# Storing a tile one step ahead of its neighbour's loads, and reordering maxima, rounding and latents at the start of an int8 stage

## The reference

```python
x = x + L0_ffn(L0_cond(x))                       # x1
y = conv(x, weight, groups=4, pad=4) + ctx + bias
outlier = any(abs(y) > 6, axis=rows)              # per column
row_absmax = max(abs(where(outlier, 0, y)), axis=1)
Cx = round(where(outlier, 0, y) * 127 / row_absmax)
out = Cx @ CB.T * (row_absmax / 127) * (SCB / 127) + outlier part + bias
x = x + out                                       # x2
```

## Time and profile before

| | us |
|---|---|
| median of three runs | 1683.25 |
| the runs | 1673.1, 1683.25, 1688.26 |
| the profiled execution | 1679.22 |
| its span, first to last instruction | 1677.5 |

### The profile page before, as it was taken

The page is one execution under the profiler, slowest core; times in us unless marked ns, Lnnn a source line. Parts: engine busy times, 40 slices in busy tenths (PEclk is TensorE's granted clock), DMA queues, the critical chain, the costliest instruction groups (busy, mean ns, idle before and its releaser), DMA issues.

```text
span 1677.5 us, 20601 instructions
## 1 busy us (share of the span) xinstructions
PE 1583.9 (94%) x7752; PEld 1289.1 (77%) x7752; DVE 833.7 (50%) x1318; ACT 506.1 (30%) x761; POOL 312.6 (19%) x262
## 2 busy tenths in 40 slices
PE   7898777999999879998999999999999999999996
PEld 5787546988987558886888888887878888888875
DVE  4666368986475545773333333333733333333336
ACT  4443223343336541223222222212242222222112
POOL 1000011134326550021311101112012111111110
PEclk9999898999999999999999999999999999999998
DMA  8765423556675667795271111112924411111115
GB/s 303 215 191 165 131 75 114 179 177 222 201 246 163 248 216 262 274 377 172 84 141 41 48 50 50 50 51 75 360 93 103 98 50 50 50 50 50 51 38 175
DMA packets 117240, 238.56 MB, mean 142 GB/s; under 512 B 22503, under 2 KB 61551, under 8 KB 115778
## 3 DMA queue, kind: packets, MB, share of 16 engines
q1 hardware_dynamic: 82042, 155.27, 27.8%
q0 software_dynamic: 23008, 68.24, 13.7%
q10 hardware_dynamic: 12112, 14.00, 2.8%
HBM read 164.51 MB, written 89.19 MB: 151 GB/s over the span
## 4 chain that ended last, share of the span: by engine, by line
PE 76%; DVE 5%; POOL 2%; issue 2%; DMA 2%; ACT 1%; SPq 0%; ACTq 0%; DVEq 0%; POOLq 0%
PE pu L1924 26%; PE pd L1924 25%; PE l_po L1924 6%; PE pf L1924 6%; POOL scratch_pairs L1433 2%; PE pw L640 2%; PE pw L639 2%; PE l_ea L1286 2%; PE l_ea L1857 1%; PE l_po L1857 1%; PE pg L1066 1%; PE l_tr L1872 1%; DMA delta<-scratch_expert_out 1%; PE l_ea L1872 1%; DVE y1T L942 1%
## 5 line engine op out<-in xcount | busy, mean ns | idle before, releaser
L1924 PE MATMUL pd<-down_hi,hid_hi 128*128 128x512 f32 x640 | 249.2, 389 | 2.9 <-issue 2.9
L1924 PE MATMUL pu<-y_hi,up_hi 128*128 128x512 f32 x640 | 249.3, 389 | 0.0
L1924 PE MATMUL pu<-y_lo,up_hi 128*128 128x512 f32 x640 | 249.1, 389 | 0.0
L1924 PE MATMUL pd<-down_hi,hid_lo 128*128 128x512 f32 x640 | 249.0, 389 | 0.0
L1924 PE MATMUL pd<-down_lo,hid_hi 128*128 128x512 f32 x640 | 249.0, 389 | 0.0
L1924 PE MATMUL pu<-y_hi,up_lo 128*128 128x512 f32 x640 | 249.0, 389 | 0.0
L2225 DVE TENSOR_TENSOR hid_lo<-hidden,hid_hi 128x512 fp32r<-128x512 f32 x64 | 44.3, 692 | 388.2 <-ACT hid_hi L2133 388.2
L2055 POOL TENSOR_TENSOR down_lo<-raw,down_hi 128x1024 fp32r<-128x1024 f32 x40 | 100.3, 2508 | 678.4 <-ACT down_hi L2070 678.4
L2127 ACT ACTIVATE hidden<-pu 128x512 f32<-128x512 f32 x64 | 38.3, 598 | 467.6 <-PE pu L1924 467.6
L2164 DVE TENSOR_TENSOR acc<-pd,acc 128x512 f32<-128x512 f32 x224 | 143.6, 685 | 54.8 <-PE pd L1924 51.5
L1924 PEld LDWEIGHTS pd<-down_hi,hid_hi 128*128 128x128 f32 x640 | 120.2, 188 | 28.6 <-issue 3.7
(11 more groups left out here) (317 smaller groups left out, 2508.7 us busy)
## 6 DMA issues: line engine op xcount, KB each, us to landing
X<-scratch_x SPq DMA_DIRECT2D x256, 64.0 KB, 2.5
l_x<-scratch_x SPq DMA_DIRECT2D x32, 512.0 KB, 6.3
delta<-scratch_expert_out SPq DMA_DIRECT2D x32, 512.0 KB, 6.9
raw<-in_up SPq DMA_DIRECT2D x32, 512.0 KB, 3.7
raw<-in_down SPq DMA_DIRECT2D x32, 512.0 KB, 4.5
y1T<-in_x SPq DMA_DIRECT2D x16, 512.0 KB, 9.6
scratch_x<-y1T SPq DMA_DIRECT2D x16, 512.0 KB, 3.2
scratch_x<-l_x SPq DMA_DIRECT2D x16, 512.0 KB, 5.6
```

The source lines that it names most:

```text
L1924: mm = pe.matmul(out, lhs[a], rhs[b], start=first and n == 0, stop=last and n == len(pairs) - 1)
```

## The change

On SP, the loop of the first stage stores tile s and only then loads the windows of tile s - 1. For tiles 14 and 15 SP loads the even pieces, ScalarE the odd ones. At the int8 stage, `row_peaks` has two `tensor_tensor` maxima in place of one `tensor_reduce`; group 0's magnitudes have room for both halves; tile 0 is scaled, rounded and split before tile 1 is rounded, into buffers of its own for tile 1 (`z_one`); group 1's magnitudes and first maxima stand earlier; 16 of the 32 latent units stand behind tile 0's, 1's and 2's products. The slots of `x2` are swapped, and GpSimd waits for the first `z_lo`.

```diff
@@ phase_first, sync @@
-            for t in range(NT):
-                sp.wait_ge(x1_made, 2 * (t + 1))
-                sp.dma_start(SC["x1"][t], x[:, t, :]).then_inc(x1_stored[t % 4], 16)
-                for c in SPLIT_AT.get(t, ()):
-                    sp.wait_ge(turned, 2 * (c + 1))
-                    x_in(LEAD + c)
-                sp.wait_ge(x1_stored[t % 4], 16 * (t // 4 + 1))
...
-                load_windows(sp, SC["x1"], t, X[t % XS], X_loaded[t % XS])
+            for s in range(NT + 1):
+                if s < NT:
+                    sp.wait_ge(x1_made, 2 * (s + 1))
+                    sp.dma_start(SC["x1"][s], x[:, s, :]).then_inc(x1_stored[s % 4], 16)
+                    for c in SPLIT_AT.get(s, ()):
+                        sp.wait_ge(turned, 2 * (c + 1))
+                        x_in(LEAD + c)
+                t = s - 1
+                if t >= 0:
+                    sp.wait_ge(x1_stored[t % 4], 16 * (t // 4 + 1))
...
+                    load_windows(sp, SC["x1"], t, X[t % XS], X_loaded[t % XS], range(0, KC, 1 if t < NT - 2 else 2))
@@ phase_first, scalar @@
                     act.copy(whT[:], pm[:, 2 * P:3 * P]).then_inc(whT_made, 1)
+                t = {NT - 1: NT - 2, NT + 1: NT - 1}.get(s)
+                if t:
+                    act.wait_ge(x1_stored[t % 4], 16 * (t // 4 + 1))
+                    act.wait_ge(conv_done, 2 * (t - XS + 1))
+                    load_windows(act, SC["x1"], t, X[t % XS], X_loaded[t % XS], range(1, KC, 2))
@@ phase_l1 @@
+    z = [buf["z_one"] if t == 1 else buf["z"][t % 2] for t in range(NT)]
...
+    PEAKS = 5
+    whole = [KC * t + KC if t < GROUPED[0][1] else KC * (GROUPED[0][1] + group_of[t]) for t in range(NT)]
@@ gpsimd @@
+        pool.wait_ge(z_lo, 1)
@@ scalar: magnitudes @@
-            if i:
-                act.wait_ge(peaked, 3 * g + 1)
-            elif g:
-                act.wait_ge(peaked, 3 * g - 1)
+            if g:
+                act.wait_ge(peaked, PEAKS * g + 2 if i else PEAKS * g - 1)
+            m0 = n * i if g == 0 else 0
@@ scalar, in program order @@
-        ahead["war"](act)
         act.wait_ge(kept, 2)
         magnitudes(0, 0)
+        magnitudes(0, 1)
+        ahead["war"](act)
         latent_out(0)
+        magnitudes(1, 0)
         latent_out(1)
-        magnitudes(0, 1)
         latent_out(2)
+        high(0)
+        high(1)
         latent_out(3)
-        latent_out(4)
-        high(0)
-        latent_out(5)
         for s in range(NT):
-            if s == 0:
+            if s == 1:
+                latent_out(4)
+                latent_out(5)
+            if s == 2:
                 latent_out(6)
-                latent_out(7)
...
+            if s == 2:
+                latent_out(7)
-            if s + 1 < NT:
+            if 1 <= s < NT - 1:
                 high(s + 1)
@@ vector: row_peaks @@
-            dve.tensor_reduce(peak[:, i, 0:n, :].unsqueeze(3), mag[:, 0:n, :, :].rearrange("k t p j -> k t j p"), AX.X,
-                              ALU.max).then_inc(peaked, 1)
+            half = mag[:, n * i:n * i + n, :, :] if g == 0 else mag[:, 0:n, :, :]
+            at = PEAKS * g + 2 * i
+            dve.tensor_tensor(half[:, :, 0:2, :], half[:, :, 0:2, :], half[:, :, 2:4, :], ALU.max).then_inc(peaked, 1)
+            dve.wait_ge(peaked, at + 1)
+            dve.tensor_tensor(peak[:, i, 0:n, :], half[:, :, 0, :], half[:, :, 1, :], ALU.max).then_inc(peaked, 1)
@@ vector, in program order @@
-        scale(0, 0, 4)
-        round_(0, 0, KC)
+        scale(0, 0, 1)
+        round_(0, 1)
+        scale(0, 1, 2)
         low(0)
+        round_(1, 1)
+        row_peaks(1, 0)
+        low(1)
@@ tensor @@
-        latent(0, 13)
+        latent(0, 6)
         turn(0)
-        latent(13, 18)
+        latent(6, 10)
         broadcast(0)
-        latent(18, 32)
+        latent(10, 16)
...
+            if s == 2:
+                latent(28, 32)
...
+            if s == 0:
+                latent(16, 19)
+                broadcast(1)
+                latent(19, 24)
+            if s == 1:
+                latent(24, 28)
```

More of the change, by code:

```diff
@@ L641, in conv_windows, with load_windows @@
     return last
-def load_windows(sp, dram, t, dst, sem):
+def load_windows(sp, dram, t, dst, sem, parts=range(KC)):
     view = dram.rearrange("t (n c) (p k) -> t p c n k", n=2 * GROUPS, p=KC)
-    for p in range(KC):
+    for p in parts:
         sp.dma_start(dst[p * GI:(p + 1) * GI, :, :], view[t, p]).then_inc(sem, 16)
@@ L729, in phase_l1 @@
     base_hi, base_lo = K["l2_base"]
-    x1, x2, bias, z, y2, stage, mag, peak, row, tmp, pf, pv, pt, pb, pg = [buf[n] for n in (
-        "x1 x2 bias z y2 stage mag peak row tmp pf pv pt pb pg").split()]
+    x1, x2, bias, y2, stage, mag, peak, row, tmp, pf, pv, pt, pb, pg = [buf[n] for n in (
+        "x1 x2 bias y2 stage mag peak row tmp pf pv pt pb pg").split()]
+    z = [buf["z_one"] if t == 1 else buf["z"][t % 2] for t in range(NT)]
     gout, g_stored = K["g_out"], K["g_stored"]
@@ L743, in phase_l1 @@
     LATE = 8
+    PEAKS = 5
     group_of = [g for g, (t0, n) in enumerate(GROUPED) for _ in range(n)]
-    first = {t0: g for g, (t0, n) in enumerate(GROUPED)}
+    whole = [KC * t + KC if t < GROUPED[0][1] else KC * (GROUPED[0][1] + group_of[t]) for t in range(NT)]
     def store_y2(sp, t):
@@ L876, in scalar @@
                     g = group_of[s] + 1
-            if g and j == 0:
+            if g and j == 0 and s:
                 magnitudes(g, 0)
@@ L935, in scale, with round_ @@
                                   pb[:, j * P:(j + 1) * P].unsqueeze(1).to_broadcast([P, KC, P]), ALU.mult).then_inc(scaled, 1)
-        def round_(g, p0, p1):
-            t0, n = GROUPED[g]
+        def round_(t0, n):
             dve.wait_ge(scaled, t0 + n)
-            for p in range(p0, p1):
+            for p in range(KC):
                 part = y[:, t0:t0 + n, p, :]
@@ L947, in low @@
                 dve.wait_ge(f_mm, 2 * (t - 1))
-            dve.wait_ge(rounded, KC * (group_of[t] + 1))
-            dve.tensor_tensor(z[t % 2][1][:], y[:, t, :, :], z[t % 2][0][:].bitcast(F32), ALU.subtract).then_inc(z_lo, 1)
+            dve.wait_ge(rounded, whole[t])
+            dve.tensor_tensor(z[t][1][:], y[:, t, :, :], z[t][0][:].bitcast(F32), ALU.subtract).then_inc(z_lo, 1)
         def add(t, h):
@@ L954, in add @@
                 dve.wait_ge(xb, t + 1)
-                if t == 0:
-                    dve.wait_ge(g_mm, KC)
+                if t == 1:
+                    dve.wait_ge(g_mm, 6)
                 if t >= 2:
@@ L959, in add @@
             dve.wait_ge(f_mm, 2 * t + h + 1)
-            dve.scalar_tensor_tensor(out=x2[:, t % 2, half], in0=pf[h][:], scalar=row[:, t:t + 1], in1=K["scb_row"][:, half],
+            dve.scalar_tensor_tensor(out=x2[:, (t + 1) % 2, half], in0=pf[h][:], scalar=row[:, t:t + 1], in1=K["scb_row"][:, half],
                                      op0=ALU.mult, op1=ALU.mult).then_inc(x2_part, 1)
             dve.wait_ge(x2_part, 2 * t + h + 1)
-            dve.tensor_tensor(x2[:, t % 2, half], x2[:, t % 2, half], x1[:, t % 2, half], ALU.add).then_inc(x2_made, 1)
+            dve.tensor_tensor(x2[:, (t + 1) % 2, half], x2[:, (t + 1) % 2, half], x1[:, t % 2, half], ALU.add).then_inc(x2_made, 1)
         dve.tensor_reduce(cmax[:].unsqueeze(2), K["top"][:].rearrange("p t k -> p k t"), AX.X, ALU.max).then_inc(kept, 1)
@@ L1031, in turn @@
             t0, n = GROUPED[g]
[L1032 removed]
+            pe.wait_ge(peaked, PEAKS * (g + 1))
             if g:
@@ L1051, in product @@
             for k in range(KC):
-                last = split_product(pe, pf[h][:], [v[:, k, :] for v in z[t % 2]],
+                last = split_product(pe, pf[h][:], [v[:, k, :] for v in z[t]],
                                      [K["cbT"][:, k, h * HALF:(h + 1) * HALF]], k == 0, k == KC - 1)
@@ L1101, in tensor @@
                 turn(g)
-            if g and ((n == 2 and j == 0) or (n == 4 and j == 1)):
+            if g and n == 4 and j == 1:
                 broadcast(g)
@@ L2382, in build @@
         phase_first(nc, K, A, SC)
+        z_one = [place(nc, UPPER, f"z_one_{part}", 194496 + 4 * D * i, [P, KC, P], F32R) for i, part in enumerate(("hi", "lo"))]
         with ExitStack() as both:
```

32 lines of the change are left out of this document (15 added, 17 removed).

## The result

The changed kernel takes 1659.7 us (median of 4 runs, 1654.3 to 1664.4) beside 1681.1 for the kernel before (4 runs, 1673.1 to 1688.3). The ratio is 0.9873, 95% interval 0.9844 to 0.9903: a gain of 21.4 us, from 16.3 to 26.2. The forecast was 1653, or 28 less, within 1640 to 1668. The sign and the places were right, the size nearly 7 us too large.

A forecast was written before the change was run, and what follows sets the result against it. TensorE, busy 94%, bounds the kernel; gains come from its waits and low clock at two seams. First seam 10.8, second 16.2, later maxima 1 sum to 28.0 off 1679.2: 1651.2, or 1655.3 by the median; forecast 1653, range 1640 to 1668.

The forecast's parts named there:

- First seam, the tail (12.3): End of the first stage: SP's tile period stops being the limit, convolution 15 moves from 191.3 to 179.0, 12.3 us gained.
- the new wait: Before convolution 12: its copy stands behind ScalarE's four loads of tile 14, a wait of some 3 us.
- nothing or 2.2: First seam: possible loss in us to the lower clock if the wait before convolution 12 brings a slow start.
- First seam, the front (1.5): Steps 1 to 3: window loads stand behind the next tile's store and two input tiles, 1.5 us lost, from 0.
- windows behind input tiles: Rival: the first four convolutions each come late, the first seam gives only 3 to 5 us, 1660; chance 0.12.
- the slower rival: Convolutions 0 to 3 each wait up to 7.5 us for windows behind input tiles, 30 in all, 1692; chance 0.03.
- Second seam (14.4): Start of the int8 stage, 198.2 to 278.1: tile 3's product starts 65.5 us behind it, not 79.9, 14.4 gained.
- the block: VectorE's split of tile 1 and group 1's maxima are held up by GpSimd's two additions, charged 3.2 us.
- the rule that I cited: VectorE and GpSimd share one port pair under an exclusive lock; VectorE operations with two SBUF inputs take part.
- Slow clock behind product 3 (+1.8): Tile 3's product in the int8 stage no longer starts at the lower clock behind a wait: 1.8 us gained.
- Shorter maxima in later groups (+1): Groups 2 to 4 of the int8 stage: shorter VectorE maxima gain 1 us, from -1 to 3.

The follow-up runs named there:

- combined: `fc_later` with GpSimd's first bias additions held back until group 1's maxima are joined: 1648.8 us, ratio 0.9828 to the kernel before.
- input_order: Changed kernel, but in steps 0 to 3 SP issues the two input tiles behind the window loads: 1656.7 us, ratio 0.9855 to the kernel before.
- fc_later: `input_order` with GpSimd's two 1 MB loads of latent weights asked for three tiles later: 1651.5 us, ratio 0.9826 to the kernel before.
- int8_seam: Changed kernel with the first stage as before, so only the int8 stage's change: 1663.7 us, ratio 0.9896 to the kernel before.
- reduce: Changed kernel with one `tensor_reduce` per half in place of the two `tensor_tensor` maxima: 1663.2 us, ratio 0.9888 to the kernel before.
- first_seam: Kernel before with only the first stage's change (SP's loop, ScalarE's half loads): 1672.3 us beside 1680.6, ratio 0.9949.

## Why the prediction was right, and where its size was off

**What bounds it: right.** Both seams were TensorE's waits, and nothing behind them took the gain back: what follows product 3 is as long as before within its scatter.

**First seam, the tail (12.3): right in mechanism, 10.4 in the trace.** SP's period, the new wait and its place came as forecast. Missing were a wait of 0.75 before convolution 11 and the 1.5 for convolution 12 at the lower clock, which I had named ("nothing or 2.2") and not counted. `combined`, with no slow start, shows 31.6 from convolution 9 to 15 against the 30.9 forecast.

**First seam, the front (1.5): the term that was mis-sized.** "I take 1.5, near the bare issue" measured 3.0 at convolution 0 and 3.4 by convolution 9. (Convolution 0's slow start costs 1.5 more and waits of 1.1 that the kernel before had are gone.) I priced two issues of input tiles alone. The first load is issued 3.7 later, most of that the wait for x1 of tile 1, and the last window lands 4.9 later, since issue and landing take longer too (8.5 us from the first issue to the copy, with the DMA share at 1.1); 1.9 of the 4.9 were slack. The stretch average, 0.60 from 82 on the earlier trace rows, hid how full the queues are: in the trace of before the share is already 0.99 from 76 to 88. `input_order` shows both parts: the order freed convolution 0, and the 1 MB load, as `fc_later` shows, then held convolution 2. The rival *windows behind input tiles* had the direction, but gave the first seam 3 to 5, so 7 to 9 lost, where 3.4 are; the slower rival needed 7 us at each of four tiles, and the one wait here is 3.6.

**Second seam (14.4): 10.8 in this trace, 13.9 in `int8_seam`.** Of the 3.6 missing, 1.6 lie ahead of product 0: the store of the first latent took 9.8 to land and held ScalarE until 16.7 behind the barrier, not 14.8. That landing varies, from 7.0 to 10.0: product 0 came at 18.3 to 20.3 in the ten traces with the new int8 stage. One more is the block, 4.1 on the rounding and not 3.2 on split and maxima. The last 1.0 is the sum of rows between `turn(1)` and product 3: 35.5 forecast, 36.5 measured, and 35.4 to 37.8 in the other traces with the short maxima. It left out `turn(2)`, which stands ahead of product 3, and three waits of 0.3 to 0.6, 1.9 together, and had the half product at the lower clock with the latents behind it 1.4 too long; a last 0.5 is spread over the other rows.

That the block strikes "just where VectorE does the split of tile 1 and these maxima" was wrong in this trace and in `reduce`, and right in the five others whose pair of additions stands there: one maximum and the split took 4.2 more, `turn(1)` came at 29.2 to 31.0 with a wait of 7.0, against a forecast of 30.0 and 7.7. What the block costs TensorE there is 2.5, against 3.2 (from 7.0 to 4.4 where it is avoided). That the rounding can be a victim too I left out, since I took from the rule that I cited only the case of two SBUF inputs; yet the row that I called "partly blocked", a rounding of 6.18 beside a pair of additions from 219.92 to 224.63, had shown it.

**Slow clock behind product 3 (+1.8): right in kind.** It is 1.00 in the stretch where it was 0.98. The second half of that product starts 5.8 behind the first and not 7.4, so 1.6 gained, of which 1.0 is left at the end of the stretch.

**Shorter maxima in later groups (+1): not seen.** TensorE waits 0.4 of 81.9 there, where it waited none.

Summed: 7.0 + 10.8 + 1.0 = 18.8 in this pair of traces, against 28.0; the times say 21.4. With product 3 at 67.0, the mean of the six traces, it is 20.8. The kernel before has one trace for its 79.8, and `first_seam` shows that it can be 2.3 less. What stays open is why the first store of x1 and the part behind product 3 differ by up to 4.6 and 6.5 us between executions, and which transfers hold the tail's last windows: no run took traffic away there.

## What to carry to other kernels

When a load is moved behind other loads, its price is not only the issue time of what it now follows: ask first what that neighbour itself waits for, then how long the landing takes with the queues as full as they are in exactly those microseconds, and look for a transfer by another engine that nobody needs yet. When work is moved to where GpSimd computes, list every VectorE instruction in that time, not only the ones that the change rewrites, and take more than one trace: a shift of 1 us changes which of them is hit and what it costs. And before removing a wait of 3 us, move it once: here two of them only went to a later tile.

## What the hardware showed unexpectedly

- Eight loads of 64 KB take SP 3.6 to 4.7 us to issue in the trace before the change (eleven of sixteen tiles under 3.8), and 3.8 to 5.7 in that of the changed kernel. Why is not shown; the mean DMA share did not rise (0.60 and 0.57 in the first of the four stretches).
